# Two of the four projection pairs of a chunk's first group moved from behind the loop's jump to ahead of it

## The reference

```python
x = coords @ fc0_w + fc0_b                       # the projection: 3 -> 32 channels
for sw, cw, cb in four layers:
    x1 = irfft2(einsum(rfft2(x)[:20, :20], sw))  # spectral convolution
    x2 = einsum("bchw,oc->bohw", x, cw) + cb
    x = gelu(x1 + x2)
x = gelu(x @ fc1_w + fc1_b)
return (x @ fc2_w + fc2_b)[..., 0]
```

## Time and profile before

| | |
|---|---|
| median of 3 runs | 6377.65 us (6371.56 to 6384.46) |
| the profiled execution's own time | 6386.84 us |
| its span | 6384.2 us |
| mean granted TensorE clock | 0.941 of full speed |
| PE busy | 5610.3 us, 88% of the span |
| DVE, ACT, POOL busy | 2860.9, 2677.3, 1103.1 us |
| the program with the eight chunks | up to about 4935 us of the span |

### The profile page before, as it was taken

How to read it: one execution, slowest core, us unless ns; L and a number is a source line. 1 busy time by engine, 2 the same in 40 slices (tenths; PEclk the granted TensorE clock), 3 DMA queues, 4 the chain that set the end, 5 groups by cost and what they waited for, 6 DMA issues and landing times. The chain is left out here.

```text
span 6384.2 us, 264603 instructions
## 1 busy us (share of the span) xinstructions
PE 5610.3 (88%) x114606; PEld 4187.0 (66%) x114606; DVE 2860.9 (45%) x4430; ACT 2677.3 (42%) x5007; POOL 1103.1 (17%) x1049
## 2 busy tenths in 40 slices
PE   5999999999899989989989999999998688888888
PEld 4787777677767876777677767767875334333343
DVE  2443344344434443444344434434443565657573
ACT  2334433433353335333433443344334546555553
POOL 3220222032203221221222122203220000000000
PEclk9999999999999999999999999999999788888887
DMA  2111111111111120111021111111110000000000
GB/s 33 14 14 14 19 14 14 14 19 14 14 16 17 14 24 8 15 24 14 9 24 14 14 19 14 14 14 16 14 14 4 19 1 8 1 8 1 4 1 4
DMA packets 442956, 84.77 MB, mean 13 GB/s; under 512 B 437592, under 2 KB 437864, under 8 KB 441704
## 3 DMA queue, kind: packets, MB, share of 16 engines
q1 hardware_dynamic: 441832, 67.58, 8.4%
HBM read 63.33 MB, written 4.23 MB: 11 GB/s over the span
## 5 line engine op out<-in xcount | busy, mean ns | idle before, releaser
L217 POOL COPY x_T<-x_X 128x512 f32<-128x512 f32 x1024 | 1073.9, 1101 | 3675.7 <-ACTq L758 3504.8
L753 ACT ACTIVATE x_X<-ga 128x512 f32<-128x512 f32 x1280 | 751.4, 597 | 1076.9 <-PE ga L452 868.2
L617 DVE COPY x_X<-ev 128x512 f32<-128x512 f32 x640 | 440.7, 689 | 979.2 <-PE ev L471 933.3
L452 PEld LDWEIGHTS ga<-pw_rhs,x_X 64*64 64x64 f32 x32768 | 592.3, 135 | 283.0 <-issue 281.8
L617 DVE COPY V<-ev 104x512 f32<-104x512 f32 x608 | 420.3, 691 | 478.3 <-PE ev L418 253.5
L483 PEld LDWEIGHTS ev<-dft_consts,x_T 128*64 128x64 f32 x16384 | 578.6, 137 | 42.9 <-issue 42.9
L483 PE MATMUL ev<-dft_consts,x_T 128*64 128x80 f32 x16384 | 599.9, 234 | 5.5 <-POOL x_T L217 3.2
L452 PE MATMUL ga<-pw_rhs,x_X 64*64 64x64 f32 x32768 | 585.5, 218 | 5.2 <-issue 5.0
L444 PE MATMUL ga<-V,inv_w 40*64 40x512 f32 x4096 | 549.0, 603 | 29.5 <-ACT V L721 27.9
L617 DVE COPY Y<-ev 128x400 f32<-128x400 f32 (+1 forms) x768 | 462.9, 603 | 211.9 <-PE ev L483 168.7
L617 DVE COPY D<-ev 128x512 f32<-128x512 f32 x576 | 362.0, 684 | 307.6 <-PE ev L390 307.6
(11 more groups left out here) (200 smaller groups left out, 8630.1 us busy)
## 6 DMA issues: line engine op xcount, KB each, us to landing
mix_w<-in_sw SPq DMA_DIRECT2D x128, 400.0 KB, 8.1
coords<-in_coords SPq DMA_DIRECT2D x64, 96.0 KB, 2.1
maps<-Y SPq DMA_DIRECT2D x128, 16.0 KB
raw<-maps SPq DMA_DIRECT2D x8, 256.0 KB, 3.5
out<-out_t SPq DMA_DIRECT2D x8, 256.0 KB, 3.5
w<-in_w SPq DMA_DIRECT2D x3, 512.0 KB, 6.5
fc_rhs<-in_fc_w SPq DMA_DIRECT2D x32, 0.4 KB
dft_consts<-in_dft SPq DMA_DIRECT2D x1, 336.0 KB
```

The lines of the kernel that those rows point to most:

```text
L217: pool.tensor_copy(x_T[:, :, H * bc + h0:H * bc + h0 + 16].rearrange("p c (s n) -> p c s n", n=2), blocks.rearrange("p (s a n c) -> p a c ...
L452: last = pe.matmul(ps[HALF * bp:HALF * bp + HALF, HALF * s:HALF * s + HALF], x_X[r:r + HALF, g, col:col + HALF], pw_rhs[r:r + HALF, :], st ...
L617: dve.tensor_copy(dst, src).then_inc(ev_taken, 1)
L753: x_new = act.activation(blocks.rearrange("p (s a n) -> p s a n", s=8, a=2)[:, :, bc, :], ga[n % N_GA][:, :].rearrange("p (s n) -> p s n", ...
```

## The change

PE's stream now issues pairs 0 and 1 of a chunk's group 0 behind `fc2(3)` of the chunk in front, ahead of the jump; pairs 2 and 3 stay behind the jump. Chunk 0 gets its pairs 0 and 1 from a new phase "lead" ahead of the loop. After the last chunk the two pairs are issued too, with nothing to use them; SP gets two more DMAs of coordinates for them, at its end, with a wait in front and a wait behind.

```diff
@@ SP, at its end
             chunk_loads(nchunk - 1, False)
+
+            sp.wait_ge(ga_taken, (nchunk - 1) * GA_CHUNK + (NG - 2) * (NB + TURN_S) + NB + 1)
+            load_coords(0, 0)
+            sp.wait_ge(coords_in[0], (nchunk * (NG // 2) + 1) * 32)
             sp.wait_ge(stored, 16 * J * nchunk * NG + 16)
@@ PE
             def run(kind, chunk, ev0, ga0, layer):
-                n = {"ev": 0, "ga": 0} if kind == "first" else {"ev": MIX_V, "ga": MIX_S}
+                n = {"ev": MIX_V, "ga": MIX_S}
+                if kind != "mid" and kind != "last":
+                    n = {"ev": 0, "ga": 0 if kind == "lead" else NB // 2}
@@
-                def project_coords(g, part):
+                def project_coords(g, part, ahead=0):
                     if part[0] == 0:
-                        pe.wait_ge(coords_in[g % 2], (chunk * (NG // 2) + g // 2 + 1) * 32)
+                        pe.wait_ge(coords_in[g % 2], ((chunk + ahead) * (NG // 2) + g // 2 + 1) * 32)
@@
                 v_at = None
+                if kind == "lead":
+                    project_coords(0, range(NB // 4))
+                    return
@@
                 if kind == "first":
-                    project_coords(0, range(NB // 2))
+                    project_coords(0, range(NB // 4, NB // 2))
                 if kind == "last":
@@
                     behind()
+                    ga0 = ga0 + GA_LAST
+                    n["ga"] = 0
+                    project_coords(0, range(NB // 4), ahead=1)
                     return
@@
+            run("lead", 0, 0, 0, None)
             phases(pe, run)
```

## The result

| | kernel before | with the change |
|---|---|---|
| median of five runs, us | 6377.65 (6365.68 to 6384.46) | 6348.43 (6332.04 to 6358.73) |
| profiled execution, us | 6386.84 | 6358.73 |
| its span, us, and mean clock | 6384.2, 0.941 | 6356.9, 0.940 |

The ratio is 0.9953, with an interval of 0.9936 to 0.9971: 30 us less, or between 18 and 41. I had forecast 6364.2, 13 us less, and a range that ended at 6353.0. The direction was right and the size was not: the measured gain is about twice the forecast, and outside the range.

What follows compares the result with a forecast made beforehand. PE, busy 88% of the span, was taken as the bound, standing 3.02 us at the first jump. Seven jumps' -18.4 us and the end's +4.9 gave -13.5 on the median 6377.65: 6364.2 us, range 6353 to 6379.

Steps and rivals of the forecast that it cites:

- The jump: PE's taken jump back to the chunk's head, seven times: starts 0.5 us later, beside eight queued matmuls, taking 3.6 to 3.8 us.
- F: Start of `fc2(3)` in front of a jump; time from there to `forward_w` measures a jump, mean 17.42 us before.
- rival of the held jump: PE's stream is held until the pairs have run, gaining only 0.5 us a jump: 6379 us, chance 0.09.
- rival that only the end is paid: PE doesn't wait for the jump, so only the program end's 4.9 us extra is left: 6382.6 us, chance 0.03.
- What is late next: After the move ACT waits for its table until F + 2.5; POOL starts at F + 3.36, allowing `forward_w` at F + 13.5.
- The gap: PE's standing time between the projection's early and later pairs at a jump: shrinks from 3.02 to about 1.8 us.
- How often the clock falls: PE's clock drops to half at five of seven jumps, `forward_w` then at F + 15.3: mean 14.8, gain 18.4 us over seven.
- The end: Behind the last stores, late idle coordinate loads and PE's two unused pairs make the program end 4.9 us later.
- The sum: Whole kernel: -18.4 us at the seven jumps and +4.9 at the end, -13.5 us, giving 6364.2 us.
- The range: Whole kernel's time between 6353 and 6379 us, taking in the first four cases, 0.91 before the scatter of the runs.
- clock staying up at all seven: Rival: no half clock at any jump, POOL the limit everywhere, 27.4 us gained less 4.9: 6355 us, chance 0.17.
- slower case: Rival: half clock lasts until about F + 18 at every jump, losing 1.5 us each: 6393 us, chance 0.06.

Runs made afterwards that it cites:

- e7: The change with the idle load early, plus two idle matmuls behind the two pairs: median 6323.87 us, ratio 0.9926 to the kernel before.
- e1: The change run again without edits, beside the kernel before: median 6362.60 us, ratio 0.9962.
- e2: The change with the idle load of coordinates moved from the end to the last chunk's phase first: median 6352.46 us, ratio 0.9947 to the kernel before.
- e6: Same kernel as e2, run again in another set: median 6332.57 us, ratio 0.9946 to the kernel before.
- e11: The change once more without edits, one run: 6343.07 us.
- e9: The kernel before, unchanged, for a second profile, one run: 6352.02 us.
- e10: The kernel before, unchanged, for a third profile, one run: 6360.24 us.
- e4: The change with one pair ahead of the jump in place of two: median 6377.23 us, ratio 0.9989 to the kernel before.
- e8: e7 plus ten empty instructions in PE's stream behind the jump, ahead of pair 2: median 6325.05 us, ratio 0.9936 to the kernel before.
- e12: e7 plus four idle matmuls at the end of the inner loop's passes: median 6347.21 us, ratio 0.9980 to the kernel before.
- e5: The change with three pairs ahead of the jump in place of two: median 6356.53 us, ratio 0.9986 to the kernel before.
- e3: The kernel before with four idle matmuls behind fc2(3), ahead of the jump: median 6374.80 us, ratio 0.9992 to the kernel before.

## Why the prediction was right in the mechanism and wrong in the size

*The jump.* Forecast: put off by 0.5 us, starting 0.6 after F, and running beside the eight queued matmuls. Measured: start F + 0.56 at all seven. Right, and with it the rival of the held jump falls; only with a third pair is the stream held. The row that I leaned on was read loosely, though: 11 records of L364 are five or six matmuls, at two records each. It takes the other tile's and those of L348 too, 19 records that start behind the inner loop's jump, to come to more than eight. The rival that only the end is paid falls too. It had stood on the 108 ns for a compare-and-branch in the Trainium skill, Advanced Engine Details and Errata, Control Flow Timing; the seven jumps of PE took 3,309 to 3,986 ns here.

*What is late next.* ACT's table, then POOL: forecast start F + 3.36, measured F + 3.19 to 3.44. `forward_w` with the clock up: forecast F + 13.5, measured 13.3 to 13.6, and 13.3 to 13.6 in e7. Right.

*The gap.* Forecast 1.8 us from the median jump of 3,690 ns in the earlier trace rows (that median counts the jump that isn't taken; the seven taken have 3,711). Measured 1.33 at the first jump, 1.16 to 1.84 over the seven. The jumps were shorter than in that one profile: 20 of 35, over the five profiles with the change's two pairs and no filler (the change, e1, e2, e6, e11), took under 3.5 us. That isn't the change's doing: the kernel before had medians of 3,426 and 3,394 ns over the jumps taken in e9 and e10.

*How often the clock falls. This is the step that failed, as far as is known.* I chose five of seven, with a mean length that puts `forward_w` at F + 15.3, between two rows of the inner loop that disagreed. Over those 35 jumps the clock fell at 15, three of seven, and ten of these lasted only 3.4 us. The way from a stretch's length to the time was nearly right: 3.4 us gives F + 13.6 to 13.9 (forecast 14.1), 6.8 gives F + 15.3 to 15.6 (forecast 15.3), and no stretch lasted 10.2. With my own three times and the counted falls the mean is (20 x 13.5 + 10 x 14.1 + 5 x 15.3) / 35 = 13.93, for seven 97.5. I forecast 103.5; the mean of the five profiles is 96.5. So six of the seven us between are this one choice. The two rows that I had weighed stood behind a different passage of work, and a gap alone doesn't settle it, as e4 and e8 show below.

*The end.* Forecast +4.9, measured +5.1, and e2 shows that it is the late load. Right.

*The sum.* With 97.5 in place of 103.5 my sum would have been -19.5, and the median 6358.2, inside the range. So the failed step is 6 of the 16 us between 6364.2 and 6348.4; the other 10 it doesn't explain. The three profiles of each kernel give -18.2, 0.29%. The timed ratios give -0.47% and -0.38%, -30 and -24 us. The interval of e1 holds -18; that of the first comparison reaches it at its upper end. So the two change sites account for 18 us. Whether the 6 to 12 us beyond it are more than scatter stays open: three profiles of each show no other stage that gained, and one kernel's stretches between the jumps differ by 13 to 18 us.

The other timings don't close it either. By the two places alone, against the mean of the kernel before, e2, e6, e7 and e8 gain 22 to 26 us; their ratios give 34, 34, 47 and 41, and the whole intervals of e7 and e8 (36 to 58 and 31 to 51 us) lie above what the places give. e12 goes the other way, with 26 us in the two places and 13 by its ratio. The kernel before wasn't profiled on the chip of e5 to e8, so where the excess lies isn't known.

*The range.* It took in the bounds of the unknown step but hardly the scatter. I read 6371.56 to 6384.46 in three runs as the kernel's spread; twelve runs of the change in e1 reach from 6333 to 6392. My base was also one profile, with 121.9 where the mean of three is 120.1.

*The rivals.* The clock staying up at all seven was priced at 6355 and lies nearer to the measured 6348.43 than the forecast does, but that nearness is luck, since it isn't what happened: the clock fell at three here and at 15 of 35. The slower case, clock down until F + 18, never showed: no stretch in those profiles lasted more than 6.8 us.

## What to carry to other kernels

A taken jump of PE's stream that costs microseconds can be laid beside matmuls: put in front of it the work that the slower engines are waiting for, as much as there are free tiles for and no more, since a single wait in the stream puts the whole jump behind the work again. Where such a move issues work once too often at the end, issue its load early, or the program's end pays for it. Before a range is written, look at how one stage differs between profiles of the same kernel: where a price hangs on whether the clock falls, one profile's seven jumps are a sample and not a rate.

## What the runs showed of the hardware

- The length of PE's jump varies from 3.31 to 3.99 us within one execution, and the clock goes with it: of the 35 jumps with the change's gap, 12 took 3,676 ns or more, and the clock fell at 10 of these; of the 23 shorter ones it fell at 5. The gap behind the pairs was 1.17 us with the jump of 3,314 ns at 4289.6 and 1.84 with the one of 3,986 at 2471.3.
- The gap's length alone doesn't decide whether the clock falls. With the 2.78 to 3.31 us of the kernel before it fell at 20 of 21 jumps, and with the 0.32 to 0.77 of e7 at none of 7. In between it goes both ways: with 0.88 to 1.35 us in e3 it fell at none of 7, but it fell at the fifth jump with the change, behind a gap of 1.16; with 1.87 to 2.23 in e4 at six of 7, and with 1.90 to 2.37 in e8 at none. Behind `fc2(3)` e8 has six matmuls in front of the gap, and e4 two; that this makes the difference wasn't tried by itself. Here are the fifth jumps of e4 and of e8, each with its window:

```profile
3100.41 2.39 PE L438 MATMUL ga<-fc_rhs,coords 49*128 49x512 f32 x6 [1.87 <-ACT x_X L766]
3096.42:3112.16 15.74, 13.87 (x65) 0.78 0.08 20
```

```profile
3071.94 1.56 PE L438 MATMUL ga<-fc_rhs,coords 49*128 49x512 f32 x6 [2.37 <-ACT x_X L773]
3065.72:3080.06 14.34, 11.59 (x68) 1.00 0.09 22
```

- ACT's and DVE's jumps at the same line take 45 and 56 ns, as the profile of the change shows, where PE's takes 3.3 to 4.0 us:

```profile
L184 DVEq COMPARE_BRANCH  x7: 56/56/56, 667.4 to 4291.1; - x7
...
L184 ACTq COMPARE_BRANCH  x6: 45/45/45, 1261.6 to 4287.6; - x6
```
